# Attention scores' product put between the next chunk's inverse products, matmul by matmul

## What is computed

```python
def step(S, inp):
    q_, k_, v_, b_ = inp
    u = b_[..., None] * (v_ - jnp.einsum('bhk,bhkv->bhv', k_, S))
    S = S + jnp.einsum('bhk,bhv->bhkv', k_, u)
    o = jnp.einsum('bhk,bhkv->bhv', q_, S)
    return (S, o)
...
o = delta_rule(q, k, v, beta)
o = o * jax.lax.rsqrt(jnp.mean(o * o, axis=-1, keepdims=True) + RMS_EPS) * norm_w
o = o.reshape(b, t, H * DV)
return o @ Wo
```

## Time and profile before

| what | value |
|---|---|
| median of 3 runs | 1355.93 us (1350.03 to 1358.77) |
| span of the profiled execution, first to last instruction | 1354.5 us |
| PE busy | 1305.2 us, 96% of the span |
| DVE, ACT, POOL busy | 868.2, 372.6, 336.6 us |
| mean granted TensorE clock | 0.984 |
| chunks' recurrence, first L1042 to last L1079 | 114.2 to 566.8 us |

### The profile page before, as it was taken

The page is one execution under the profiler, slowest core; times in us unless marked ns, Lnnn a source line. Parts: engine busy times, 40 slices in busy tenths (PEclk is TensorE's granted clock), DMA queues, the critical chain, the costliest instruction groups (busy, mean ns, idle before and its releaser), DMA issues.

```text
span 1354.5 us, 27271 instructions
## 1 busy us (share of the span) xinstructions
PE 1305.2 (96%) x8466; PEld 824.9 (61%) x8467; DVE 868.2 (64%) x2426; ACT 372.6 (28%) x816; POOL 336.6 (25%) x396
## 2 busy tenths in 40 slices
PE   8968999999999999999999999999999999999996
PEld 7857777887777556544444455555555555555553
DVE  4896688559667523845111477777777777777774
ACT  4745545555453223220000011111111111111111
POOL 1211214232222211313564012212222122122221
PEclk9989999999999999999999999999999999999997
DMA  4525742733456496246447555566665565664420
GB/s 158 97 45 112 109 111 68 147 96 82 98 132 156 103 238 136 81 148 219 190 179 249 174 123 109 110 173 149 134 140 130 128 138 128 129 135 74 73 50 1
DMA packets 208513, 171.05 MB, mean 126 GB/s; under 512 B 71472, under 2 KB 160560, under 8 KB 208432
## 3 DMA queue, kind: packets, MB, share of 16 engines
q1 hardware_dynamic: 135056, 114.16, 32.3%
q0 software_dynamic: 16496, 34.23, 12.8%
q10 hardware_dynamic: 56880, 21.54, 7.6%
HBM read 91.06 MB, written 82.73 MB: 128 GB/s over the span
## 4 chain that ended last, share of the span: by engine, by line
PE 53%; DVE 2%; issue 0%; POOLq 0%; DVEq 0%; ACT 0%
PE pD L2182 15%; PE pG L2162 14%; PE pU L2171 13%; PE pG L2126 3%; PE pU L2126 3%; PE pD L2145 3%; DVE ups L2072 1%; PE pU L2120 1%; PE pD L2140 0%; POOLq L1897 0%; DVE w L1784 0%; DVE w L1785 0%; DVE route_keep L1783 0%; DVE q L1803 0%; DVE qf L1796 0%
## 5 line engine op out<-in xcount | busy, mean ns | idle before, releaser
L2072 DVE STREAM_TRANSPOSE ups<-a 32x96 f32<-32x96 f32 (+1 forms) x1264 | 330.2, 261 | 42.9
L1969 POOL DMA_INDIRECT out<-y,ix x79 | 123.0, 1557 | 482.0 <-ACT y L2025 328.3
L2182 PE MATMUL pD<-w,ups 128*128 (+1 forms) x474 | 219.3, 599 | 3.6 <-DVE ups L2072 3.6
L2171 PE MATMUL pU<-w,xsT 128*128 x632 | 199.9, 459 | 0.0
L2162 PE MATMUL pG<-w,xsT 128*128 x632 | 199.9, 458 | 0.0
L2162 PEld LDWEIGHTS pG<-w,xsT 128*128 128x128 f32 x632 | 119.5, 189 | 88.4 <-issue 37.5
L2171 PEld LDWEIGHTS pU<-w,xsT 128*128 128x128 f32 x632 | 120.1, 190 | 66.9
L950 PE MATMUL pProj<-front_region 128*128 128x256 f32 x624 | 158.4, 398 | 2.0 <-ACT front_region L697 1.6
L2182 PEld LDWEIGHTS pD<-w,ups 128*128 128x128 f32 (+1 forms) x474 | 90.8, 192 | 98.0 <-issue 81.7
L1311 DVE SCALAR_TENSOR_TENSOR front_region<-front_region,cw 128x256 f32<-128x256 f32 x288 | 131.7, 498 | 14.5 <-ACT front_region L733 11.1
L950 PEld LDWEIGHTS pProj<-front_region 128*128 128x128 f32 x624 | 115.3, 194 | 21.5 <-ACT front_region L733 2.3
(11 more groups left out here) (240 smaller groups left out, 1591.8 us busy)
## 6 DMA issues: line engine op xcount, KB each, us to landing
w<-in_up_T SPq DMA_DIRECT2D x16, 1408.0 KB
slot_rows<-zeros SPq DMA_DIRECT2D x79, 266.0 KB, 6.5
xs<-slot_rows ACTq DMA_DIRECT2D x316, 64.0 KB
w<-in_down_T SPq DMA_DIRECT2D x16, 512.0 KB
front_region<-in_L_attn_hidden_states SPq DMA_DIRECT2D x16, 256.0 KB, 3.8
x2r<-in_L_attn_hidden_states SPq DMA_DIRECT2D x16, 256.0 KB, 5.0
partial_sums<-x2r SPq DMA_DIRECT2D x16, 256.0 KB, 3.6
x_normed<-x2n SPq DMA_DIRECT2D x16, 256.0 KB, 2.4
```

The source lines that it names most:

```text
L1969: pool.indirect_dma_start(out=flat, out_offset=bass.IndirectOffsetOnAxis(ap=ix[1 - par][:, 0:1], axis=0), in_=y[1 - par][:, :], in_offset= ...
L2072: dve.transpose(aT[par][B * to:B * to + B, 0:n, rows], a[rows, 0:len(IC) * P].rearrange("p (c n) -> p c n", c=len(IC))[:, 0:n, B * to:B * ...
L2171: mm = pe.matmul(pU[0][:, 0:I], xsT[par][:, k, :], w[:, bass.ds(slot, 1), 2 * I * k + I:2 * I * (k + 1)], start=(k == 0), stop=(k == DC - 1))
L2182: mm = pe.matmul(pYq[:, :], aT[1 - par][0:m, c, :], down[0:m, :, UPW + D * c:UPW + D * (c + 1)], start=(c == 0), stop=(c == 2))
```

## The change

The score product leaves `hop_o`. It is issued inside `hop_u` of the next chunk: after each matmul of the inverse product of chunk n comes one of the score product of chunk n - 1. The two chunks have opposite halves, so the two products lie in opposite quarters, and the score product takes head group 1 - f, so the other bank of pC. The last chunk's score product stands by itself in slot 1 of step 16. To fit this, the output copies move on ACT from slots 2 and 5 to slot 4 of the same step and slot 1 of the next; `o_square` moves from the end of slot 0 to slot 2, `o_sums` and `o_norm` from slot 1 to slot 2. `oT_turn` stays in slot 3, now behind the other transposes of that slot. PT gets three buffers for two.

```diff
-                    if s == 1 and tile_ok(u - 1):
+                    if s == 2 and tile_ok(u - 1):
                         o_norm(u - 1)
...
                     if tile_ok(u) and s in (2, 5):
                         s_copy(u, s // 3)
-                        o_copy(u, s // 3)
+                    if s == 2 and tile_ok(u - 1):
+                        o_square(u - 1)
...
                         u_copy(u, s // 3)
+                    if s == 1 and tile_ok(u - 1):
+                        o_copy(u - 1, 1)
+                    if s == 4 and tile_ok(u):
+                        o_copy(u, 0)
...
-                    if s == 0 and tile_ok(u - 1):
-                        o_square(u - 1)
...
+            def score_product(t, c, n, f):
+
+                r, g = cols(c, C), HH * f + n
+                return pe.matmul(pC[r, f, cols(n)], PT[t % PT_RING][r, cols(g)], Us[r, cols(g)], start=False, stop=True,
+                                 skip_group_check=True)
+
+            def wait_scores(t, c):
+                pe.wait_ge(s_PT, t + 1)
+                pe.wait_ge(s_U, 2 * t + c + 1)
+                pe.wait_ge(s_QS, 2 * t + c + 1)
+
             def hop_u(t, c):
...
+                tp, cp = divmod(2 * t + c - 1, 2)
+                if tp >= 0:
+                    wait_scores(tp, cp)
                 pe.wait_ge(s_R, 2 * t + c + 1)
                 r = cols(c, C)
                 for n in range(HH):
                     for f in range(2):
                         g = HH * f + n
-                        mm = pe.matmul(pC[r, f, cols(n)], TT[t % TT_RING][r, cols(g)], Rs[r, cols(g)], start=True, stop=True)
-                mm.then_inc(s_Up, 1)
+                        u_mm = pe.matmul(pC[r, f, cols(n)], TT[t % TT_RING][r, cols(g)], Rs[r, cols(g)], start=True, stop=True)
+                        if (n, f) == (HH - 1, 1):
+                            u_mm.then_inc(s_Up, 1)
+                        if tp >= 0:
+                            o_mm = score_product(tp, cp, n, 1 - f)
+                if tp >= 0:
+                    o_mm.then_inc(s_Op, 1)
...
-                for f in (c, 1 - c):
-                    if f != c:
-                        pe.wait_ge(s_QS, 2 * t + c + 1)
-                    for n in range(HH):
-                        g = HH * f + n
-                        mm = pe.matmul(pC[r, f, cols(n)], PT[t % 2][r, cols(g)], Us[r, cols(g)], start=False, stop=True,
-                                       skip_group_check=True)
-                mm.then_inc(s_Op, 1)
...
+                    if (u, s) == (NT, 1):
+                        last_scores(NT - 1, 1)
...
                     if s == 3:
-                        if tile_ok(u - 1):
-                            oT_turn(u - 1)
...
                             xT(2 * new)
+                        if tile_ok(u - 1):
+                            oT_turn(u - 1)
...
-                    if s == 1 and tile_ok(u - 1):
+                    if s == 2 and tile_ok(u - 1) and (even or not pair_ok(pq)):
                         o_sums(u - 1)
```

More of the change, by code:

```diff
@@ L45 @@
 FIRST, LAST = -8, NT + 3
-KQ_RING, KT_RING, VH_RING, NP_RING, TT_RING, ACC_RING = 4, 7, 5, 6, 4, 6
+KQ_RING, KT_RING, VH_RING, NP_RING, TT_RING, ACC_RING, PT_RING = 4, 7, 5, 6, 4, 6, 3
 FRONT_W = DC * D * 3 + 3 * DC * (HALO + PW) + 2 * D + 2 * DC * PW + ACC_RING * PW + DC * PW + 2 * HB * HB
@@ L254, in attention @@
     TT = [sb(f"TT{i}", [P, H * C]) for i in range(TT_RING)]
-    PT = [sb(f"PT{i}", [P, H * C]) for i in range(2)]
+    PT = [sb(f"PT{i}", [P, H * C]) for i in range(PT_RING)]
     LX, LT = route["keep"][:, 0:HB * HB], route["keep"][:, HB * HB:2 * HB * HB]
@@ L742, in silu @@
                 else:
-                    least(act, s_Op, 2 * (2 * (p - KQ_RING) + 2))
+                    least(act, s_QS, 2 * (2 * (p - KQ_RING) + 2))
                     out = kq[p % KQ_RING][:, i % DC + (DC if i >= 2 * DC else 0), :]
@@ L1055, in hop_u, with last_scores @@
                         g = HH * f + n
-                        mm = pe.matmul(pC[r, f, cols(n)], TT[t % TT_RING][r, cols(g)], Rs[r, cols(g)], start=True, stop=True)
-                mm.then_inc(s_Up, 1)
+                        u_mm = pe.matmul(pC[r, f, cols(n)], TT[t % TT_RING][r, cols(g)], Rs[r, cols(g)], start=True, stop=True)
[5 more added lines that the diff above has]
+                    o_mm.then_inc(s_Op, 1)
+            def last_scores(t, c):
+                wait_scores(t, c)
+                for n in range(HH):
+                    for f in range(2):
+                        mm = score_product(t, c, n, f)
+                mm.then_inc(s_Op, 1)
             def hop_o(t, c):
-                pe.wait_ge(s_PT, t + 1)
                 pe.wait_ge(s_ktc, t + 1)
@@ L1362, in mask_scores @@
                 dve.wait_ge(s_Pp, t + 1)
-                least(dve, s_Op, 2 * t - 2)
-                dve.tensor_tensor(half_major(PT[t % 2][:, :]), two_banks(pG),
+                least(dve, s_Op, 2 * (t - PT_RING) + 2)
+                dve.tensor_tensor(half_major(PT[t % PT_RING][:, :]), two_banks(pG),
                                   causal[:, :].unsqueeze(1).unsqueeze(1).to_broadcast([P, 2, HH, C]), ALU.mult)\
@@ L1644, in _ @@
                             scale_gram(2 * pq)
+                        if s == 2 and tile_ok(u - 1):
+                            o_sums(u - 1)
                         if s in (0, 2, 4):
```

## The result

The changed kernel takes 1374.55 us, the median of 4 runs (1372.95 to 1375.96). The kernel before takes 1356.68 in the runs beside it (1350.03 to 1358.77). The ratio is 1.015, interval 1.0129 to 1.0171: slower by 1.5%, and above the range of the prediction. The profiled execution has a span of 1373.8 us and a mean granted clock of 0.971, where before it was 1354.5 and 0.984.

A forecast was written before the change was run, and what follows sets the result against it. PE was taken as the bound through attention, jointly with DVE in seven half tiles. Gain -27.9, full DVE +6.3, stalls +21.9 and clock +2 made +2.3 on 1355.93, so 1358 us, range 1341 to 1370.

The forecast's parts named there:

- The gain of 27.9 us (31 x 0.9): PE's list in attention: score product overlaps the inverse product fully less one pass, 0.9 us for each of 31 chunks.
- The rule on banks: Inverse and score products in PSUM: passes meeting in one bank would go one by one, 0.46 us a chunk, +14.
- The clock, 2 us: PE's new pauses in attention: one or two stretches of 3.4 us at half clock, 1.7 us each, taken as 2 us.
- rival (b): Every new pause at `oT_turn` answered by half clock, 1.7 us more each, 8 further stretches, 14 us: 1372; chance 0.13.
- The stalls of 21.9: PE waiting at `oT_turn` for the late output chain, summed over attention's steps: 21.9 us, between 12 and 30.
- DVE's 6.3 us: Seven half tiles where DVE is full: a faster PE only waits sooner, 7 x 0.9 us of the gain go.
- The arithmetic of step 12: Output chain in step 12: result at 479.85 against 477.42 wanted, so PE waits 2.4 to 2.5 us; steps 12 to 14 alike.
- 2.1, 1.4 and 2.0 net: Stall terms at `oT_turn` in steps 10, 11 and 15, after deducting what DVE waits absorb or already took.
- the 1.3 and 0.7 that I took: Stalls per odd step: 1.3 us each in steps 1, 5 and 9, 0.7 each in steps 3 and 7.
- the old wait for Rs: Steps 3 and 7: PE's old 1.89 us wait for DVE takes up most of the new one, leaving 0.7 each.
- (a): Output chain covered after all, only full DVE takes something, half the stalls at most left: -19, 1337; chance 0.13.
- (c): The two quarters don't overlap as read, 27.9 shrinks to half or nothing, stalls stay: 1372 to 1386; chance 0.10.

The follow-up runs named there:

- e4: The changed kernel with the score product on the same head group as the inverse product beside it, so both write one bank of pC: 1374.07 us, ratio 1.0134.
- f1: The kernel before, with the interleaving for tiles 11, 12 and 13 only and their square in slot 1: 1350.27 us, ratio 0.9973.
- g1: The kernel before, with POOL's power repeated 5, 6 and 5 times in tiles 11, 12 and 13, so PE pauses before the transposes: 1372.22 us, ratio 1.0113.
- g2: g1 with 8 products of zeros ahead of PE's wait in those three steps: 1368.22 us, ratio 1.0085.
- e2: The changed kernel with 8 products of zeros on PE ahead of the wait for the normalised output, from tile 9 on: 1361.78 us, ratio 1.0054.
- e1: The changed kernel with the output's square on ACT in slot 1, right behind the copy of the tile's second chunk: 1358.91 us, ratio 1.0027.
- e5: The changed kernel with the normalised output sent to an unread scratch tile and the transposes waiting for the output copies alone: 1350.44 us, ratio 0.9966.
- f2: The kernel before, with the interleaving and the square in slot 1 for tiles 1, 3, 5, 7, 11, 12 and 13 only: 1347.25 us, ratio 0.9945.
- e7: e1 with 8 products of zeros ahead of the wait for the normalised output in steps 10, 11 and 15: 1350.36 us, ratio 0.996.
- e3: The changed kernel with the score product as a block of 8 behind the 8 inverse products, not between them: 1390.2 us, ratio 1.0268.

## Why the prediction was wrong

**The gain of 27.9 us (31 x 0.9) was right.** A group costs 0.93 us less, with full overlap; the account above uses 28.8. The rule on banks that stood against it did not apply (e4).

**The clock, 2 us, is the step that failed.** I took one or two new stretches of 3.4 us at half clock. There were some 54 us of it in attention in place of 22, worth 16 us. My own rows held the warning, and rival (b) drew the conclusion: 14 us, 1372. I held it for unlikely (0.13) because the pause of 1.89 us had no such answer. That was the luck of one execution. The same wait in step 7 stands, with nothing changed ahead of it, in the traces of f1, g1 and g2, each time 1.89 us long, and in all three the clock falls 2.3 to 2.9 us after it begins. In g1:

```profile
345.70 1.51 PE L1058 MATMUL pC<-Rs,TT 64*64 64x64 f32 x15 [1.89 <-DVE Rs L1375]
```

```profile
346.08:349.49 3.41, 3.41 (x16) 2.22 (x15) 3.34 (x5) 0.59 (x1) 0.00 (x0) 0.50 0.07 17
```

In the changed kernel's trace the pauses of 2.27 us and more were followed by half clock, all nine. Rival (b) named 2.5 us as its point, and my sum put three pauses exactly there. e2 shows that this cost is real and separate, 12.8 us. The 16 us come from the account and not from a single experiment, and up to 3.4 of them belong to the pause of step 13.

**The stalls of 21.9 and DVE's 6.3 us were too small.** Together 28.2, and PE's idle time grew by 35.8, the pause of step 13 included. The arithmetic of step 12 was right: 2.29, 2.27 and 2.39 us in steps 12 to 14 for 2.5. e1 shows the moved square to be their cause. Three steps were mis-sized. Steps 10, 11 and 15 have 3.69, 4.39 and 5.89 us, where I had 2.1, 1.4 and 2.0 net. In step 11 the sums stand on DVE behind two parts of the inverse and another reduction: square at 446.55, sums at 449.33, a distance of 2.78 us where step 12 has 0.65. In step 15 it is POOL. Its timeline there:

```profile
567.52 1.16 POOL L634 TENSOR_SCALAR ro<-so 128x8 f32<-128x8 f32 x1 [8.28 <-DVE so L1412]
568.76 1.00 POOL L635 TENSOR_TENSOR ro<-ro,qe 128x8 f32<-128x8 f32 x1
569.84 2.64 POOL L636 TENSOR_TENSOR ro<-ro,nhalf 128x8 f32<-128x8 f32 x1
572.56 1.88 POOL L638 TENSOR_TENSOR osb<-osb,ro 128x512 f32<-128x512 f32 x1
```

The same four instructions take 6.9 us, where step 12 has 3.4. The trace of the kernel before held a part of this: in its step 15 they take 4.7, from 550.60 to 555.28. I had priced the chain once and used the price everywhere.

**The shape of the odd and even steps.** Steps 1, 3, 5, 7 and 9 have 1.60, 1.84, 1.36, 1.85 and 1.76 us of wait, more than the 1.3 and 0.7 that I took; steps 2, 4, 6 and 8 have 0.69, 0.02, 0.49 and 0.02 for 0.4. That the old wait for Rs would absorb part of the new one in step 7 came true: 0.2 us are left of 3.3.

**Rivals.** (a), the chain is covered: no, 31.8 us of waits. (c), no overlap: no. (b) was right in its mechanism and nearly in its number. By my terms a kernel without the stalls would take 1355.93 - 27.9 + 6.3 = 1334. e5 measured 1350: waits for DVE and the clock keep most of the gain there too.

**What stays open.** Why the third pause in g1, and one of 3.4 us in step 1 of e2, had no fall of the clock behind them. Why there is time at half clock without a long pause ahead: the kernel before has 3.4 us of it at 296.1 us, with no pause over 1.1 us in the 60 us before, and at 234.6 and 360.9 us, some 7 us after pauses of 1.2. And what the pauses without a releaser are (2.85 us in the changed kernel, 2.26 in g2). One thing about them stands in the traces: there are 16 such pauses of over 1.1 us between 107 and 600 us in the twelve traces, and in each case a 16 KB packet of DMA queue 8, which carries instructions, had landed 1.3 to 2.1 us before PE went on (in the changed kernel it landed at 502.62, PE went on at 504.03). Such packets come every 11 us on average. That suggests that PE was waiting for its own program; no run varied it, so it isn't shown.

## What to carry to other kernels

Work taken off the bounding engine's list is a gain only where nothing else is due at the same time: read, stretch by stretch, who is late next, and price a chain over several engines anew in each stretch, since the same instructions can stand in another queue or last twice as long there. Price a new pause of TensorE at its length plus what the granted clock does behind it; here the three added pauses of g1 cost 1.7 times their length, and the half clock behind the nine of the changed kernel (28.5 us long in all, 44 us at half clock) made them up to 1.8 times as dear. If such a change has to make something wait, apply it only to the tiles where the chain is covered (f2), or give the engine something to do ahead of the wait (e2, e7).

## What the runs showed of the hardware

Two 64x64 fp32 products in opposite quarters of the array run as fast as one: pairs of passes start within 0.01 us, a pair each 0.058 us, 32 passes in 0.93 us. Whether a pair writes one bank or two made no difference (e4).

Pauses of PE and the granted clock, between 107 and 600 us in all twelve traces: of 52 pauses of 2.2 us or more 45 were followed by half clock within 5 us of their start, of 14 between 1.89 and 2.2 us 5. The same pause can be followed or not: the wait of 1.89 us in step 7 three times of four, the waits of 2.3 to 2.4 us at `oT_turn` in steps 12 to 14 three of three in the changed kernel and in e4, one of three in e3. Pauses of 2.84 us (g1), 2.94 (f2) and 3.39 (e2) were not followed so. With products of zeros, 2.05 us of them ahead of the wait, three of the five pauses of over 1.8 us that were left had no fall behind them, and the other two (2.75 and 3.91 us, e2) had it later, after 4.8 us, and for 3.4 us.

POOL's small instructions took longer where DVE was busy with wide ones: L634 takes 0.25 us in step 12, where DVE is idle, and 1.16 in step 15, beside DVE's wide tensor_tensor of 1.22 us; L638 1.04 and 1.88. The Trainium skill (GPSIMD Engine Reference, Specifications) says that the two share their interfaces to SBUF and contend when DVE's instruction has two inputs there. The trace agrees; no run here varied it.
